# A graph, mixer and LSTM layer on one core: loads and zero pieces reordered, variances kept by node, prefix and suffix folded

## The reference

```python
xn = layernorm(x)
# graph part
h = (1 + eps) * xn + segment_sum(xn[src], dst)
h = relu(h @ W1 + b1) @ W2 + b2
gnn = (h - mean(h, 0)) * rsqrt(var(h, 0) + 1e-5) * gamma + beta
# mixer: 8 heads of 32, all nodes one sequence
q, k, v = split(xn @ w_qkv + b_qkv)          # per head
k, v = ln(k, kln_g, kln_b), ln(v, vln_g, vln_b)
kv = einsum('nd,ne->de', k, v) / N           # per head
mix = gelu((q @ kv + xn) @ w1 + b1) @ w2 + b2 + xn
x = x + gnn + mix
# recurrence over the 6250 nodes in order, 256 wide
out = lstm(layernorm(x))
g = argmax(out @ W_lin.T + b_lin)            # 0 or 1 per node
w = g * out
inc = cumsum(w)
x = x + 2 * out + (inc - w) * fw_att + (inc[-1] - inc) * bw_att
```

## Time and profile before

| | us |
|---|---|
| median of 3 runs (16857.71 to 16862.74) | 16860.86 |
| the profiled execution | 16838.88 |
| its span, first to last instruction | 16837.2 |

### The profile page before, as it was taken

How to read it: one execution, slowest core, us unless ns; L and a number is a source line. 1 busy time by engine, 2 the same in 40 slices (tenths; PEclk the granted TensorE clock), 3 DMA queues, 4 the chain that set the end, 5 groups by cost and what they waited for, 6 DMA issues and landing times. The chain is left out here.

```text
span 16837.2 us, 921205 instructions
## 1 busy us (share of the span) xinstructions
PE 12623.9 (75%) x375188; PEld 11631.8 (69%) x375188; DVE 10192.6 (61%) x84227; ACT 5185.6 (31%) x32373; POOL 2589.9 (15%) x1609
## 2 busy tenths in 40 slices
PE   3333344468888888888888888888888888888887
PEld 2222233348888888888888888888888888888886
DVE  4433211266666666666666666666666666666667
ACT  1000000133333333333333333333333333333333
POOL 4888888600000000000000000000000000000000
PEclk6666666675555555555555555555555555555555
DMA  5444444410000000000000000000000000000000
GB/s 140 71 72 72 67 68 68 80 62 1 1 1 1 1 1 1 1 1 1 1 1 1 1 1 1 1 1 1 1 1 1 1 1 1 1 1 1 1 1 16
DMA packets 923352, 317.17 MB, mean 19 GB/s; under 512 B 755540, under 2 KB 875112, under 8 KB 923315
## 3 DMA queue, kind: packets, MB, share of 16 engines
q0 software_dynamic: 435200, 207.54, 8.2%
q1 hardware_dynamic: 464589, 98.59, 3.2%
q10 hardware_dynamic: 23526, 10.59, 0.3%
HBM read 150.06 MB, written 150.93 MB: 18 GB/s over the span
## 5 line engine op out<-in xcount | busy, mean ns | idle before, releaser
L1261 PE MATMUL bank<-hrest,whh 128*128 128x1 bf16 (+1 forms) x300000 | 9077.1, 166 | 1920.3 <-DVE hrest L1385 1920.3
L1261 PEld LDWEIGHTS bank<-hrest,whh 128*128 128x128 bf16 x300000 | 8548.9, 104 | 2481.0 <-DVE hrest L1385 2480.6
L1329 ACT ACTIVATE gates<-bank 128x4 f32<-128x4 f32 x12500 | 2183.5, 175 | 8141.6 <-DVE bank L1366 7254.0
L1366 DVE TENSOR_REDUCE bank<-bank 128x4 f32<-128x12 f32 x12500 | 2210.0, 177 | 3186.0 <-PE bank L1261 2300.4
L1261 PE MATMUL bank<-xsteps,wih 128*128 128x15 bf16 (+1 forms) x60048 | 2714.9, 174 | 0.0
L1374 DVE CUSTOM_DVE_ANT_1 uv<-gates 128x4 f32<-128x4 f32 x12500 | 2041.3, 163 | 450.1
L1261 PEld LDWEIGHTS bank<-xsteps,wih 128*128 128x128 bf16 x60048 | 2277.1, 104 | 0.0
L1337 ACT ACTIVATE bank<-gates 128x1 f32<-128x1 f32 x12500 | 2176.9, 174 | 124.8
L1390 DVE TENSOR_TENSOR hrest<-hrest 128x1 f32<-128x1 f32 x12500 | 1987.4, 159 | 216.2
L1395 DVE TENSOR_TENSOR hrest<-hrest 128x1 f32<-128x1 f32 x12500 | 1961.2, 157 | 217.1
L1261 PE MATMUL bank<-ones,gbias 128*128 128x5 bf16 x10008 | 1678.6, 168 | 18.6 <-DMA xsteps<-x_d 18.6
(11 more groups left out here) (167 smaller groups left out, 3726.3 us busy)
## 6 DMA issues: line engine op xcount, KB each, us to landing
acc_d<-zero SPq DMA_DIRECT2D x40, 637.5 KB, 14.5
ht<-acc_d SPq DMA_DIRECT2D x100, 224.0 KB
xsteps<-x_d SPq DMA_DIRECT2D x1252, 7.5 KB, 1.7
U<-hrest SPq DMA_DIRECT2D x1250, 5.0 KB, 1.7
rows<-xn_d,staged_i POOLq DMA_INDIRECT x800, 4.0
acc_d<-sums,target POOLq DMA_INDIRECT x800, 6.1
x_d<-x SPq DMA_DIRECT2D x25, 375.0 KB, 2.3
xk<-U SPq DMA_DIRECT2D x50, 125.0 KB, 5.0
```

The costliest lines, as they stand in the source:

```text
L1261: return nc.tensor.matmul(to, w, v, start=start, stop=True, skip_group_check=True)
L1329: nc.scalar.activation(gates[:, k, 0:2 * NG_[k]:2], zi[k], ACT.Tanh).then_inc(ifg_act[k], 1)
L1366: nc.vector.tensor_reduce(zi[k], gi[k][b][:, s], axis=AX.X, op=ALU.add).then_inc(ifg_summed[k], 1)
```

## The change

It has five parts.

- **Loads and zeros.** The ten loads that keys and values need (wkv, bkv, kv_g, kv_b) are issued by ScalarE at the start of the first block, ahead of its square root, on mixw_in; the other 14 stay at the start of the second block on a semaphore of their own, late_in, that the mixer's second block waits for. The stores of xn move from ScalarE to SP. SP writes ten zero pieces ahead of them, the other 30 in turn with the rows, after tiles 0, 2 and 4 of each five.
- **Feed-forward weights** are issued by ScalarE instead of SP.
- **Norm.** The variance is made with the squares as the stationary operand and one column of 1/256: 125x2 numbers per chunk, node on the partition. Root, reciprocal and refinement (four operations instead of five) work on 125x2; TensorE turns the result back to a row on all partitions. The three parts are float32 tiles, whose upper halves are read as bf16 (cut off, not rounded), packed as part, k, t.
- **Recurrence.** The projections read the parts as `xs_hi`, every other bf16 with the parts 40 bytes apart; the load of a block doubles from 7.5 to 15 KB.
- **Last stage.** inc-w is not made. With h the state, the forward part adds -fw*w to XT; afterwards (fw-bw)*inc + bw*last comes from ScalarE in one operation, and VectorE adds h to XT and that to the result.

```diff
@@ first block, SP
-                for a in range(NA):
-                    flat = acc_d[a].rearrange("n d -> (n d)").rearrange("(p w) -> p w", p=128)
-                    for j in range(ZS):
-                        sp.dma_start(flat[:, j * ZW:(j + 1) * ZW], zero[:]).then_inc(zero_out[a], 16)
...
+                for piece in range(ZS):
+                    zeros(piece)
+                piece = ZS
+                for t in range(NT):
+                    sp.wait_ge(xn_ready, t + 1)
+                    for lo, hi in SPLIT:
+                        sp.dma_start(xn_d[t * R + lo:t * R + hi, :], xn[lo:hi, t % XB, :]).then_inc(xn_out[t % XB], 16)
+                    if t % 5 in (0, 2, 4):
+                        zeros(piece)
+                        piece += 1
@@ first block, ScalarE
+                ld = [(wkv[:, k, s], wv[:, k, :, s + 1, :]) for k in range(KD) for s in range(2)]
+                for s in range(2):
+                    ld.append((bkv[:, s], bv[s + 1:s + 2, :, :].broadcast_to([R, HEADS, HC])))
...
+                for to, v in ld:
+                    act.dma_start(to, v).then_inc(mixw_in, 16)
@@ norm, TensorE
-                        last = nc.tensor.matmul(bank[2][:, 0:C], avg[:], csq[:, k, :], start=k == 0, stop=k == KD - 1)
+                    for j in range(2):
+                        for k in range(KD):
+                            last = nc.tensor.matmul(bank[2][0:R, j:j + 1], csq[:, k, j * R:(j + 1) * R], avg[:, 0:1],
+                                                    start=k == 0, stop=k == KD - 1)
...
+                        last = nc.tensor.transpose(bank[3 + b][:, j * R:(j + 1) * R],
+                                                   nrs[:, b, j:j + 1].broadcast_to([R, 128]), ident[0:R, 0:R])
@@ norm, VectorE: one step
+                    if more:
+                        variance(c + 1, 1 - b)
+                    if within(c + 3):
+                        residual(c + 3)
+                    if more:
+                        inverse(c + 1, 1 - b)
+                    scaled(c, n, b)
+                    if more:
+                        inverse_square(c + 1, 1 - b)
                     if within(c + 2):
+                        center(c + 2, b)
+                    if more:
+                        correction(c + 1, 1 - b)
+                    first_rest(c, b)
+                    if more:
+                        corrected(c + 1, 1 - b)
+                    second_rest(c, b)
@@ recurrence, projections
-                                yield to[:, :, 0:PARTS - p], wih[:, p, k, cols], xs_[:, b, k, :, 0:PARTS - p], False
+                                yield to[:, :, 0:PARTS - p], wih[:, p, k, cols], xs_hi[:, b, 0:PARTS - p, k, :].rearrange("p c t -> p t c"), False
@@ last stage, VectorE, forward
-                    nc.vector.tensor_tensor(XT[:, :, at], XT[:, :, at], states(c), ALU.add).then_inc(sum_ready, 1)
+                    for k in range(KD):
+                        stt(out=XT[:, k, at], in0=wgt[:, k, :], scalar=minus_fw[:, k:k + 1], in1=XT[:, k, at],
+                            op0=ALU.mult, op1=ALU.add).then_inc(base_ready, 1)
...
-                    nc.vector.tensor_tensor(pre[:], inc[:, :, at], wgt[:], ALU.subtract).then_inc(pre_ready, 1)
...
-                    for k in range(KD):
-                        stt(out=XT[:, k, at], in0=pre[:, k, :], scalar=fw[:, k:k + 1], in1=XT[:, k, at],
-                            op0=ALU.mult, op1=ALU.add).then_inc(fwd_ready, 1)
@@ last stage, output
-                        nc.scalar.activation(suf[:, b, k, :], inc[:, k, bass.ds(c * C, C)], ACT.Identity, scale=-1.0,
-                                             bias=last_inc[:, k:k + 1]).then_inc(suf_ready, 1)
+                        nc.scalar.activation(suf[:, b, k, :], inc[:, k, bass.ds(c * C, C)], ACT.Identity,
+                                             scale=diff[:, k:k + 1], bias=lastw[:, k:k + 1]).then_inc(suf_ready, 1)
...
-                        stt(out=fin[:, b, k, :], in0=suf[:, b, k, :], scalar=bw[:, k:k + 1], in1=XT[:, k, at],
-                            op0=ALU.mult, op1=ALU.add).then_inc(fin_ready, 1)
+                    nc.vector.tensor_tensor(XT[:, :, at], XT[:, :, at], states(c), ALU.add).then_inc(sum_ready, 1)
...
+                    nc.vector.tensor_tensor(fin[:, b], suf[:, b], XT[:, :, at], ALU.add).then_inc(fin_ready, 1)
```

More of the change, by code:

```diff
@@ L231, in _ @@
                 first_apart(act, NT // XB, body)
-                for b in range(XB):
-                    act.wait_ge(xn_out[b], 32 * (NT // XB))
             @block.vector
@@ L1059, in _ @@
                 variance(0)
+                mean(2, 0)
+                variance(1)
                 skewed(pe, step)
@@ L1099, in _ @@
                 batch_norm(2)
+                root(0, 0)
+                square(1, 1)
+                batch_norm(3)
                 skewed(act, step)
-                second_part(NC - 1, (NC - 1) % 2)
             @block.vector
@@ L1118, in center, with variance @@
                         dve.wait_ge(csq_ready, c - 1)
-                        dve.wait_ge(xl_ready, c - 1)
+                        dve.wait_ge(p1_ready, c - 1)
                     nc.vector.tensor_tensor(cent[:, b], XT[:, :, at], mean, ALU.subtract).then_inc(cent_ready, 1)
+                def variance(c, b):
+                    dve.wait_ge(var_made, c + 1)
+                    nc.vector.tensor_scalar(nvar[:, b, :], bank[2][0:R, 0:2], LN_EPS, None, ALU.add)\
+                      .then_inc(nvar_ready, 1)
@@ new lines, in inverse, with inverse_square, correction @@
+                def inverse(c, b):
+                    dve.wait_ge(nroot_ready, c + 1)
+                    if due(c - 1):
+                        dve.wait_ge(rows_made, c - 1)
+                    nc.vector.reciprocal(nrs[:, b, :], nroot[:, b, :]).then_inc(newton, 1)
+                def inverse_square(c, b):
+                    dve.wait_ge(newton, 3 * c + 1)
+                    nc.vector.tensor_tensor(nsq[:, b, :], nrs[:, b, :], nrs[:, b, :], ALU.mult).then_inc(newton, 1)
+                def correction(c, b):
+                    dve.wait_ge(newton, 3 * c + 2)
+                    nc.vector.scalar_tensor_tensor(out=nfix[:, b, :], in0=nsq[:, b, :], scalar=-0.5, in1=nvar[:, b, :],
+                                                   op0=ALU.mult, op1=ALU.mult).then_inc(newton, 1)
@@ new lines, in corrected, with scaled @@
+                def corrected(c, b):
+                    dve.wait_ge(newton, 3 * c + 3)
+                    nc.vector.scalar_tensor_tensor(out=nrs[:, b, :], in0=nfix[:, b, :], scalar=1.5, in1=nrs[:, b, :],
+                                                   op0=ALU.add, op1=ALU.mult).then_inc(nrs_ready, 1)
+                def scaled(c, n, b):
+                    rows_ = bank[3 + b][:, 0:C].rearrange("p (o n t) -> p o n t", o=1, t=B)\
+                        .broadcast_to([128, KD, C // B, B])
+                    dve.wait_ge(rows_made, c + 1)
+                    if due(16 * n):
+                        dve.wait_ge(x2_out[b], 16 * n)
+                    nc.vector.tensor_tensor(part(b, 0), cent[:, b].rearrange("p k (n t) -> p k n t", t=B), rows_,
+                                            ALU.mult).then_inc(p1_ready, 1)
@@ L1155, in step @@
[L1155 to L1162 removed]
+                    more = within(c + 1)
@@ L1166, in _ @@
                 center(0, 0)
+                residual(2)
+                center(1, 1)
+                variance(0, 0)
+                inverse(0, 0)
+                inverse_square(0, 0)
+                correction(0, 0)
+                corrected(0, 0)
                 skewed(dve, step)
-                first_rest(NC - 1, (NC - 1) % 2)
-                third_part(NC - 1, (NC - 1) % 2)
             @block.sync
```

205 lines of the change are left out of this document (91 added, 114 removed).

## The result

The changed kernel takes 16689.22 us (median of four runs, 16684.21 to 16702.05), the kernel before 16860.62 (16857.71 to 16862.74): a ratio of 0.990 (0.988 to 0.992), 171 us less. The forecast was 16701. The profiled execution took 16702.05, its span is 16700.1 against 16837.2, so the two profiles account for 137 of the 171 us.

| stretch | before | after | difference | forecast |
|---|---|---|---|---|
| start to first scatter | 211.1 | 187.6 | -23.5 | -57 |
| first to last scatter | 3073.2 | 3071.3 | -1.9 | 0 |
| last scatter to first accumulator sum | 20.6 | 20.0 | -0.6 | -4 |
| first sum to first new state (norm inside) | 461.0 | 357.4 | -103.6 | -92 |
| first to last new state | 12893.8 | 12911.0 | +17.2 | 0 |

What follows compares the result with a forecast made beforehand. Bound by the recurrence (12902 us) and the edge stage paced by GpSimd's gathers and scatters, both unchanged. Terms -57-4-92+0-11+4 = -160 from the median 16860.86 give 16701 us, range 16637 to 16766.

Steps and rivals of the forecast that it cites:

- Part 1: First block, loads ahead and zeros strewn: first scatter at 154, -57 us, range -37 to -86.
- (a): First block: TensorE's 57.63 us wait for mixer weights goes, about 15 us remain from block end to first scatter; -54.
- (b): End of the first block: square root at 69, rows from 70, block end at 140; 110 if early loads cost nothing.
- The sum of 31 and 36: First block: x's load (31 us) and the ten loads' issues (36) share engines and add to 67, delaying the root.
- rival A: First block: early loads only move the wait, first scatter at 201, -10 from this stage, total 16748; chance 0.15.
- Part 2: Start of the feed-forward part: SP's first accumulator load moves from 3298.65 to 3294.03; -4 us (0 to -5).
- Part 3: Norm stage: chunk period falls from 9.06 to 5.4 us, TensorE at full clock part of the time; -92 (-76 to -105).
- rival D: Norm and last stages: TensorE stays at 1.2 GHz, norm period 6.1, last stage loop-bound; -122, 16739; chance 0.05.
- rival B: First block, norm and last stages: free loads and a warm TensorE, clock near 1.0; -211, 16650; chance 0.12.
- Part 4: Recurrence: wider column spacing and a doubled block load fit the 0.31 us free per step; 0.
- Rival C: Recurrence: projections outgrow their gap and the kernel is slower, 16977 at 32 ns more each; chance 0.04.
- Part 5: Last stage: chunk period falls from 4.6 to about 4.2 us, -11; the output part's extra addition costs +4.

Runs made afterwards that it cites:

- e1: The changed kernel with each of the four norm vectors loaded once per partition instead of once per partition and head: 16660.02 us.
- e4: The changed kernel with its ten early loads, but all 40 zero pieces ahead and the row stores issued by ScalarE, as before the change: 16721.81 us.
- e9: The changed kernel with the ten early loads issued by GpSimd instead of ScalarE: 16677.27 us.
- e7: The changed kernel with the eight one-column products of the norm's variance made twice: 16723.55 us.
- e8: The changed kernel with one more pair of 128x250 products per norm-stage chunk, into a bank nobody reads: 16673.57 us.
- e11: The changed kernel with whole-row key/value loads, norm vectors once per partition, strewn zeros issued by ScalarE, and an unread wide product pair per norm chunk: 16640.97 us.

## Why the prediction was right, and where it was not

**What bounds the kernel, and the total**: right, the total in part by luck. The recurrence and the edge stage kept their times, and all of the gain is in the four places named.

**Part 1 failed by 33.5 us**, at the term "Root at 69, rows from 70, end at 70+66+4 = 140". Its (a) held: no wait for weights, and 17.5 us from the block's end to the first scatter, where 14 were forecast (3.5 of the miss). Its (b) was mis-sized three times. The root came 10 late and the first row 11 (80.9 for 70). The sum of 31 and 36 was the wrong account: x and the loads passed side by side (x's last piece at 34.18 for 31.38), and the ten issues alone took 76.5 us where I took 36 from the earlier trace rows. That 67 lay near 78.7 was luck; the packets, as e1 shows, give the time. Then came the stuck stores, 12.22 us in which VectorE stood. And rows with zeros pass at 318 GB/s here and at 313 in e1 (81 us from the first row to the block's end), where I took the 385 of the earlier trace rows for both. That 385 belongs to a stretch which is mostly zeros; zeros alone reach 391 in e4. An estimate from e1: 81 us at 313 GB/s less 19.1 MB of zeros at 391 leaves 32 us for the 6.4 MB of rows, 200 GB/s. The 19 us that the stretch from the first row to the end took beyond my 70 are thus about 11 of pace, as e1 shows, and the rest the stuck stores. The prediction named as a sign of being wrong "if the first scatter comes after 175"; on this part I was. It lay between forecast and rival A, and nearer to A (201). Of A's two causes the blocked queue is in the trace, until 77.4; x was held up by under 3 us, and by 34 only in e9.

**Part 2**, -4 forecast, -0.6 found. The first accumulator load is issued at the start of its part, at 3268.70, but the first sum follows 10.2 us later, at 3278.88; before it followed 6.3 us after an issue that stood behind the weights. I took an earlier issue for an earlier landing. Both queues now share the engines: from 3268 to 3274 the weights' queue moves 0.95 MB and the accumulators' 0.30. Some 2.5 MB pass up to the first sum, in 10.2 us, where some 2.4 MB passed in 10.9 before; what must pass did not change, only who issues it. This is read from the traces, and was not tried.

**Part 3**, -92 forecast, -104 found. The mechanism was right (e7: the loop sets the period), and two errors cancelled in part. I took weight loads beside wide products, 1.34/4 = 0.33 us each at 1.2 GHz, for loads with one column, which take 1.76/8 = 0.22: 1.8 us for the eight where the sum has 2.7. The other terms held: from the variance to the end of the centring 2.4 to 2.5 us (2.5 forecast), the square 0.62 (0.68). So the loop at 1.2 GHz is 4.9 to 5.1, where I had 6.1. And "should be granted full clock part of the time" was wrong: TensorE is busy for 108.7 of 135 us and the clock is 0.50 throughout. In this stage the clock was rival D's and the gain rival B's (-105).

**Part 4**: 0, and so it was. Rival C is out: 0.31 us for six projections and 0.31 idle, before and after. No run here shows a penalty for columns 40 B apart, where the prediction quoted a rule of the Trainium skill, "SBUF — State Buffer" (SBUF cachelines), that spoke for one.

**Part 5**, -11 and +4 forecast, -28 and +3 found. The loop terms were right (3.4 at full clock); the clock was not. I carried the old mean of 0.77 into the new stage, where it is 0.99. The far end of my range (-29) was the right one. Why this stage got that clock stays open.

The range held with 12 us below the forecast, but by cancelling. With part 1 alone wrong it would have been 16734. The stages gave 6 us less than the sum of -160, and some 17 us more, which bring the median below the forecast, lie in no stage that the profiles compare; the recurrence alone varies by 29 us between executions. (The bounds add up to 16636, not 16637.)

## What to carry to other kernels

Count a load's packets, not its bytes: ten loads of 1.3 MB in some 10,000 packets held ScalarE for 77 us, and loading the norm vectors once per partition instead of once per head gave 35 us. A load moved early needs room on the engines as well as on a queue; price it with what will run beside it there, for that is where e4's gain went. When a rewrite shortens a stage, take the clock of the new stage as unknown and price its loop at both levels.

## What was unexpected

- The same issue on ScalarE can be short or long, it seems by what is queued ahead of it: 0.39 us and 10.22 us for loads of the same shape in e1; and 38.61 us in e4 for one that took 18.39 in the changed kernel.
- Useless products made a stage faster: period 4.86 to 4.19 us with the granted clock at 0.91 for 0.50 (e8).
- In e8 and e11 a chunk of the last stage takes 3.6 us instead of 3.46, though its code is the same. From the gate's end to TensorE's first product it takes 0.43 us instead of 0.25. The cause is open, and was not tried.
